# Third layer's state-space stage: the drive that TensorE makes is put into two other PSUM banks, and its matmuls are reordered

## The reference

```
delta = softplus(einsum('btr,ir->bti', delta_raw, dt_proj_w) + dt_proj_b)
A = -exp(A_log)
h0 = zeros((B, D_INNER, D_STATE))
def step(h, inp):
    d_t, b_t, c_t, xc_t = inp
    dA = exp(A[None, None, :] * d_t[..., None])
    h = dA * h + d_t[..., None] * b_t[:, None, :] * xc_t[..., None]
    y = einsum('bis,bs->bi', h, c_t)
    return (h, y)
hT, ys = scan(step, h0, (delta, B_param, C_param, xc))
y = ys + D_param * xc
out = einsum('bti,di->btd', y * silu(z), out_proj_w)
```

## Time and profile before

| | us |
|---|---|
| median of 3 runs | 5335.22 (5332.41 to 5345.41) |
| profiled execution, its own time | 5330.66 |
| its span, first to last instruction | 5328.6 |
| busy: PE, DVE, ACT, POOL | 4395.1, 3533.3, 2766.8, 2506.6 |
| mean granted TensorE clock, share of full | 0.907 |

### The profile page before, as it was taken

The page is one execution under the profiler, slowest core; times in us unless marked ns, Lnnn a source line. Parts: engine busy times, 40 slices in busy tenths (PEclk is TensorE's granted clock), DMA queues, the critical chain, the costliest instruction groups (busy, mean ns, idle before and its releaser), DMA issues. The chain is left out here.

```text
span 5328.6 us, 109199 instructions
## 1 busy us (share of the span) xinstructions
PE 4395.1 (82%) x42504; PEld 2710.1 (51%) x42504; DVE 3533.3 (66%) x6837; ACT 2766.8 (52%) x4982; POOL 2506.6 (47%) x2343
## 2 busy tenths in 40 slices
PE   8768999999999999677854888887798879985779
PEld 6545666666666666434632343443365444423445
DVE  4347777777777777386455999999764426646646
ACT  4326666666666666463334666565464415542322
POOL 7537666666666666252164766766533310001100
PEclk8789999999999999887866999999999959996889
DMA  1010100101011000000000000000000000003000
GB/s 24 16 30 14 32 20 20 33 21 32 22 29 24 16 16 20 7 1 3 12 0 15 1 0 0 1 0 1 15 1 1 5 14 5 17 1 75 5 21 7
DMA packets 92004, 76.98 MB, mean 14 GB/s; under 512 B 30999, under 2 KB 74279, under 8 KB 90727
## 3 DMA queue, kind: packets, MB, share of 16 engines
q1 hardware_dynamic: 89447, 68.95, 5.2%
q0 software_dynamic: 2048, 1.05, 0.1%
HBM read 40.18 MB, written 1.18 MB: 8 GB/s over the span
## 5 line engine op out<-in xcount | busy, mean ns | idle before, releaser
L4220 POOL TENSOR_TENSOR l_attn_read<-l_attn_state,l_attn_c_rows 128x1024 f32<-128x1024 f32 x256 | 604.5, 2362 | 292.3 <-DVE l_attn_state L4122 174.2
L2595 PE MATMUL psum<-l_ffn_wq,l_ffn_xsT 128*128 128x512 f32 x1152 | 605.5, 608 | 106.9 <-DVE l_ffn_t L2870 101.7
L3006 POOL TENSOR_TENSOR l_ffn_t<-l_ffn_t 128x512 f32<-128x512 f32 x384 | 486.9, 1268 | 417.6 <-DVE l_ffn_t L2870 413.0
L3842 PE MATMUL psum<-l_attn_read,ident 128*128 128x512 f32 x1024 | 489.5, 596 | 7.3 <-DVE l_attn_yz L4130 5.0
L2866 DVE TENSOR_TENSOR l_ffn_t<-psum,l_ffn_tab 128x512 f32<-128x512 f32 x384 | 260.5, 678 | 324.6 <-ACT l_ffn_sq L2746 305.5
L3012 POOL TENSOR_TENSOR l_ffn_t<-l_ffn_t,l_ffn_ss 128x512 f32<-128x512 f32 x384 | 400.3, 1043 | 62.7 <-DVE l_ffn_ss L2885 62.6
L2746 ACT ACTIVATE l_ffn_sq<-psum 128x512 f32<-128x512 f32 x384 | 225.3, 587 | 288.0 <-PE psum L2595 285.6
L4122 DVE TENSOR_TENSOR_SCAN l_attn_state<-l_attn_decay,psum 128x1024 f32<-128x1024 f32 x144 | 328.9, 2284 | 4.5
L2643 PEld LDWEIGHTS psum<-l_ffn_pT,l_ffn_v 64*64 64x64 f32 x3072 | 231.8, 134 | 167.3 <-ACT l_ffn_pT L2768 133.0
L3998 ACT ACTIVATE l_attn_decay<-l_attn_dt,l_attn_a 128x1016 f32<-128x1016 f32 x256 | 292.9, 1145 | 36.0 <-DVE l_attn_state L4119 32.6
L4023 ACT COPY l_attn_c_rows<-psum 128x512 f32<-128x512 f32 x256 | 149.4, 584 | 298.5 <-PE psum L3833 260.1
(11 more groups left out here) (917 smaller groups left out, 11304.0 us busy)
## 6 DMA issues: line engine op xcount, KB each, us to landing
l_ffn_vx<-l_ffn_v SPq DMA_DIRECT2D x192, 128.0 KB, 2.3
l_ffn_wq<-in_L_ffn_Wqkv SPq DMA_DIRECT2D x6, 1536.0 KB, 6.3
l_xattn_toep<-s4d_taps SPq DMA_DIRECT2D x4, 2048.0 KB, 17.5
l_ffn_wo<-in_L_ffn_Wo SPq DMA_DIRECT2D x6, 512.0 KB, 3.9
l_ffn_w<-in_L_ffn_W SPq DMA_DIRECT2D x6, 341.0 KB
l_ffn_w<-in_L_ffn_w SPq DMA_DIRECT2D x3, 512.0 KB, 4.0
x_all<-in_x SPq DMA_DIRECT2D x4, 256.0 KB, 4.6
l_attn_k<-l_attn_dense_k POOLq DMA_DIRECT2D x64, 16.0 KB, 1.9
```

Source lines behind the costliest of these rows:

```text
L2595: nc.tensor.matmul(ring[it % 2], xsT[:, n % 2, m % G, :], w, start=True, stop=True).then_inc(itemed, 1)
L3006: nc.gpsimd.tensor_tensor(t1[:, m % G, i, :], t1[:, m % G, i, :], t2[:, x % 3, :], ALU.add).then_inc(added, 1)
L3842: last = nc.tensor.matmul(total[:, h * GT:(h + 1) * GT], K.ident[:], read[:, k % 3, h * GT:(h + 1) * GT], start=(n == 0), stop=(n == N - 1 ...
L4220: nc.gpsimd.tensor_tensor(read[:, k % 3, :].rearrange("p (h n) -> p h n", h=2), state[:, k % 3, :].rearrange("p (h n) -> p h n", h=2), row ...
```

## The change

For a step K that TensorE drives, the first half of the drive goes to bank 4, which otherwise holds B's row, and the second half to the columns of the first, bank 2. The first half now waits until VectorE has read B's row (`driven`), the second until the first half of the scan of K - 1 is done (`halved`). Bank 4 is then taken until the first half of the scan of K is done, so the row of B for K + 1 moves from iteration K - 1 to iteration K and waits for that. The scan reads from the new places.

```
+        pe_drive = (b_bank, K.psum[:, HW:HW + GT])
...
                     if k >= 1:
                         pe.wait_ge((driven, c_moved)[m], k if m else rows_before(k))
+                    if m == 0 and k >= 1 and by_pe(k - 1):
+                        pe.wait_ge(halved, split_before(k - 1) + 1)
...
                     if h == 0:
                         pe.wait_ge(diag_ready, pe_before(k) + 1)
+                        pe.wait_ge(driven, rows_before(k))
+                    else:
                         pe.wait_ge(halved, split_before(k - 1) + 1)
-                    else:
-                        pe.wait_ge(scanned, k)
                     for i in range(G):
-                        last = nc.tensor.matmul(drive[:, h * GT + i * T:h * GT + (i + 1) * T], duT[:, g % 2, h, i, :], b_diag[:, pe_before(k) % 2, i, :],
+                        last = nc.tensor.matmul(pe_drive[h][:, i * T:(i + 1) * T], duT[:, g % 2, h, i, :], b_diag[:, pe_before(k) % 2, i, :],
...
                     if k + 1 < NS and by_pe(k + 1):
+                        drive_half(k + 1, 0)
                         row(k + 1, 1)
                         add(k - 2, 0)
-                        drive_half(k + 1, 0)
                         drive_half(k + 1, 1)
-                        row(k + 2, 0)
+                        add(k - 2, 1)
+                    elif g < NG and by_pe(k):
+                        add(k - 2, 0)
+                        row(k + 1, 0)
+                        row(k + 1, 1)
                         add(k - 2, 1)
                     else:
-                        if k + 1 < NS and not (g < NG and by_pe(k)):
+                        if k + 1 < NS:
                             row(k + 1, 0)
...
-                            nc.vector.tensor_tensor_scan(state[:, k % 3, at], decay[:, k % 3, h, :, :].rearrange("p g t -> p (g t)"), drive[:, at], 0.0,
+                            source = pe_drive[h] if by_pe(k) else drive[:, at]
+                            nc.vector.tensor_tensor_scan(state[:, k % 3, at], decay[:, k % 3, h, :, :].rearrange("p g t -> p (g t)"), source, 0.0,
```

## The result

| us | before | after |
|---|---|---|
| median of 12 runs | 5334.28 | 5346.61 |
| ratio, 95% interval | | 1.0024 (1.0016 to 1.0033) |
| profiled execution, its span | 5328.6 | 5350.4 |
| stage: VectorE's first to last drive | 924.4 | 941.7 |

One of the 12 runs before, of 5874.12 us, is left out of the ratio, and without it the median before is 5333.59 and the difference 13.0 us (12.3 with it).

The account below looks back on a forecast made before the run. VectorE's stream was taken as the stage's clock, with TensorE's deliveries to it deciding. Over 56 steps the terms summed to +19.7, say +20 us, on 5335: 5355 us, forecast's own range 5346 to 5362, overall range 5333 to 5370.

Parts of the forecast that it names:

- part 1: First drive half in bank 4: ready a whole microsecond early, so the scan of K follows without a gap, removing 0.41 us.
- part 3: Row of B for K + 1, behind two halves of adds: VectorE's next drive 0.25 us later, bounds 0.15 to 0.35.
- part 4: Extra pieces in iteration K - 1, now ahead of B's row: VectorE waits for all, 0.43 us small, 0.86 large.
- part 5: Steps after a TensorE-driven one: they neither give the loss back nor add to it; TensorE needs 8.3 of 9.99 us.
- part 6: States 3 and 12 of groups 2 to 4: other VectorE work covers the row; -0.41 us each and 0.
- part 7: State 52 of groups 1 to 3: -0.4 us at low clock, -2.8 at full; the middle, -1.4 each, was taken.
- part (2): Second drive half, behind C's row and half an add: 0.08 us given back, scan of K ends 0.33 earlier.
- The old one: VectorE's wait for TensorE's drive ahead of a scan: forecast to fall from 30.1 to under 12 us.
- the row is not late: Rival at B's row: always there in time, leaving the early scan's gain; about -21 us, 5314; chance 0.13.
- The clock falls more often: Rival on TensorE's clock: ten half-clock steps would add 10 to 15 us, 5368; chance 0.1.
- The two effects nearly cancel: Rival: row late by 0.45 rather than 0.55 and state 52 at full clock; +11 us, 5346; chance 0.2.
- three classes: Whole-time outcomes: faster by over 0.3% (16 us) 0.12, within it 0.28, slower by over it 0.60.

Follow-up runs that it names:

- first experiment: Changed kernel with the row of B for K + 1 issued at the end of iteration K - 1, banks and waits unchanged: 5309.57 us, ratio 0.9946 to the kernel before.

## Why the prediction was right, and where it was off

The mechanism held step by step. The first half is ready early and the wait before the scan is gone (part 1); the row of B is late behind the adds (part 3); extras count in full (part 4); nothing is given back later (part 5); `skip` and `scale` cover (part 6); state 52 gains (part 7). The 0.08 that part (2) gave back did not come: with the row out of the way a step gains the whole 0.41 (first experiment). The new wait is where it was named, and a little larger: 51 times against "some 47", 47.3 us against 35 to 45. The old one fell to 12.8, not under 12. The wait came to 0.63, 1.07 and 1.49; against the named 0.55, 1.0 and 1.4 this is longer by 0.08 because the idle time is counted from the end of the scan, where 0.10 passes in any step.

The term that was mis-sized is that of part (3), the plain step: +0.25 forecast, +0.12 measured, for 25 steps and, inside the other classes, for 22 more. From the drive of K - 1 to that of K + 1 I had 6.58 us and it was 6.46. The halves of TensorE's drive made the difference: I took 1.01 for each, half of the whole drive before. Measured from start to start they are 3107.98 - 3107.01 = 0.97 and 3109.95 - 3109.06 = 0.89. The 2.02 was not the price of two halves alone. In the kernel before, the second half waits for the whole scan of K - 1, which ends at 3104.33 + 2.33 = 3106.66, and starts just behind it:

```profile
3106.71 1.16 PE L3872 MATMUL psum<-l_attn_b_diag,l_attn_duT 128*128 128x128 f32 x8
```

From there to the row at 3107.71 it takes 1.00. With the bank and the wait of before put back (the second half left in bank 3) it takes 1.00 again, and in the first experiment, the same but for these, 0.89. This holds for 41 of the 56 steps before and 45 with the second half in bank 3 (0.99 or 1.00), and for 45 in the changed kernel and 47 in the first experiment (0.89). So 2.02 - 0.97 - 0.89 = 0.16 of the price was the old wait, one of those that the change itself takes away.

Against that the first starts 0.15 after VectorE's drive ends, not 0.09. Together -0.10, and the allowance of 0.03 for weights was not needed; the reader followed the row 0.42 later, not 0.41, which makes it -0.12. Over 47 steps 0.13 each is 6 us, the whole surplus of the forecast and more; the half-clock stretches at state 33 and the slow start of group 1 gave some of it back (+2.64, +1.28, +1.43 and +0.95).

State 52 was taken as the middle between -0.4 and -2.8. It scattered over that span and a little beyond, -1.97, -0.28, -1.50 in one profile and -0.57, -1.39, -1.72 in the other; that the three came to -3.8 for -4.2 is luck, since neither end was derived to be the likelier. Granted clock around the first of them, in the changed kernel:

```profile
3092.00:3096.00 4.00, 1.28 (x9) 1.09 (x9) 3.96 (x4) 3.97 (x5) 2.35 (x1) 1.00 0.00 0
3096.00:3100.00 4.00, 3.62 (x12) 2.50 (x13) 2.10 (x2) 4.00 (x8) 2.72 (x1) 0.57 0.00 0
```

TensorE is busy 1.28 of 4 us at 2.4 GHz, and then, with the work back, for the most part at 1.2 GHz. The earlier first half did not keep the clock up, as before.

The rivals: "the row is not late" is refuted by the new wait itself, and the first experiment shows what it would have been worth, -26 us against its -21. "The clock falls more often" came true at state 33, where it is worth 2.4 of the 17 us. "The two effects nearly cancel" had 5346, and the median is 5346.61, which is also the lower end of the forecast's own 5346 to 5362. That agreement is luck. One half of this rival came, a row that is less late (by 0.13 a step, where it had 0.10), the other did not: state 52 gave 3.8 us and not 8.4. In the stage the sum is +17.3, nearer to the forecast's 20 than to its 11, and only what scatters outside the stage brings the median to its number. The chances of the three classes do not follow from those of the rivals either: added up these give 0.13, 0.32 and 0.55, where I wrote 0.12, 0.28 and 0.60.

## What to carry to other kernels

When a buffer is freed by borrowing another, ask what the lender was used for next: here a row that was never on the path was put behind 1.7 us of adds and any extra, and cost more than the wait that was won. In a stream that is issued in order, the first question for each moved instruction is who reads it and what now stands ahead of it. The remedy was one line further up, and it turned +17 us in the stage into -26, some 2.5 of which are a clock that came out full at two steps. And a price read off a trace can hold a wait inside it: here a drive of 2.02 us had 0.16 of a wait that the change removed.

## What the runs showed of the hardware

Scans of 128x512 without a wait between them start 1.11 to 1.14 us apart though each lasts 1.19 to 1.22; a wait for another engine costs this overlap too. A wait that the profile gives as 0.30 was worth 0.41 when it went, and one of 0.14 (the second half left in bank 3) cost 0.25.

Eight records of a drive half take 0.89 us from start to start when TensorE comes to them without a wait, 0.97 after idle time of 0.98 or 1.42 us, and 1.00 when they had to wait for the end of a scan just ahead.

At state 33 of the first group the granted clock is 0.74 in the changed kernel, 1.00 in the kernel before and 1.00 in the first experiment, over the 6.5 us from the drive of state 32. What TensorE did in the 6 us ahead was the same in the first two, at full clock in both. Before:

```profile
3004.71:3010.71 6.00, 4.17 (x11) 1.34 (x9) 5.79 (x4) 3.70 (x8) 4.09 (x4) 1.00 0.00 0
```

After:

```profile
3016.23:3022.23 6.00, 4.17 (x11) 1.35 (x9) 5.79 (x4) 3.70 (x8) 4.09 (x4) 1.00 0.00 0
```

So these rows do not show why it falls in the one and not in the other. It is no accident of a single execution: in the second profile of each kernel the clock is 0.74 at the same states 33 and the steps differ by +2.64, +1.32 and +1.43.
